# An earlier start of the first q and v products, and attention's scores as three fp32r passes in place of one fp32 product

## The chip, the cores and the metric

The kernel runs on one core of a Trainium2 chip. The metric is the device time of one execution in microseconds (us). The core's engines run their own instruction streams and meet at semaphores: PE (TensorE, the products), DVE (VectorE), ACT (ScalarE), POOL (GpSimd) and SP (SyncE, which only issues transfers here). PEld is PE's loading of weights, shown apart.

## The reference, cut to what matters

An input of 8 batches x 512 rows x 128 goes through four layers: attention, a mixture of 16 experts, a state-space layer, and the experts again. The change is in the first one:

```python
x = x + attn(layernorm(x), w_qkv, w_proj, b_proj)
# attn: q, k, v = split(x @ w_qkv.T); one head of width 128 for the scores
scores = einsum('bqh,bkh->bqk', q, k) * scale      # 512 x 512 per batch
probs  = softmax(scores);  out = probs @ v
out    = out @ w_proj.T + b_proj
# then: x = x + ffn(layernorm(x)), whose router takes the top 4 of 16 experts
```

## The kernel before, in words

All work is ordered by hand: each engine's block is a list of steps, and every step names the semaphores that it waits for. Attention is a software pipeline over the 8 batches (`skewed`, L269): step i, from -1 to 7, holds on every engine the work of four batches at once: the layer norm and the q and v products of batch i+1 (`first`), the scores and softmax of batch i (`second`), the projection and the router's norm of batch i-1 (`third`), and the router's logits, top 4 and weights of batch i-2 (`fourth`). Step -1 is the start-up. Pieces of weight preparation (`prep`) are mixed into steps -1 to 1. After step 7 the expert layer begins (`ffn_all`), which keeps PE busy until the state-space layer.

Since q.k = x Wq' Wk x', one matrix `a_qk` is made once, "q" is `a_qk` times the transposed normed input `xnT` (`q_proj`, L1582), and the scores are one product of 128x128 by 128x512 for each of 4 row blocks r, with `xnT` as the other side (`scores`, L1564). The names by step and engine, in the order of a step's chain:

- DVE: `ln1_stats` (L1050, L1053) of batch i+1, two `maxes` (L1065), `xn_out` (L1059), the third max, `x1_out` (L1075), `router_stats` of i-1 (L1081, L1084), the fourth max, `router_lg` and `router_top` of i-2 (L1103 to L1121), `recip` (L1070), `router_weights` of i-2 (L1128 to L1140), `router_norm` (L1090) and `router_xn` (L1096) of i-1. Then the next step's L1050.
- POOL: `ln1_chain` (L460, L462), which `xn_out` waits for; `add_bias` (L468), which waits for `xn_out`; `router_stash` of i-2 (L454), which writes the low part `ffn_lo` for the expert layer; `router_chain` of i-1 (eight of L434, one of L449), which waits for `router_stats` and which `router_norm` waits for.
- ACT: `router_t` (L659, L661), two `exps` (L623), two `pT` (L629), `xnT_out` (L636), two more `exps`, `q_out` (L641), two `pT`, `router_exp` (L666), `attn_out` (L652), `router_out` (L670), `v_out` (L646).
- PE: scores 0 and 1 (L1569), `router_turn` (L1626), scores 2, `project` (L1617), scores 3, `p_turn` 0 and 1 (L1599), `xn_turn` (L1579), `router_logits` (L1633), `pv` 0 (L1609), `q_proj` (L1584), `p_turn` 2, `v_proj` (L1593), `p_turn` 3, `pv` 1 to 3, `router_parts` (L1639).

The tiles `qT` and `xnT` have two slots, used in turn. At the start, small vectors (biases and the like) come by six small transfers into one row, and a product with a column of ones (L1850) spreads them over the partitions; ACT copies them to `vecs` (L854).

In the start-up step PE's list was, word for word:

```python
xn_turn(0)
eng.wait_ge(w_vecs, 6 * 16)
eng.matmul(bank(2)[:, 0:VEND], ones[0:1, :], vec_row[0:1, 0:VEND], ...).then_inc(prep_ps, 1)
eng.wait_ge(prep_sb, 2)
q_proj(0, 0); prep(0, 0); v_proj(0, 0); prep(0, 1)
```

The functions that the diff touches, and what calls them:

## Time and profile before

| | us |
|---|---|
| median of 3 runs | 724.89 |
| lowest and highest | 724.85, 726.3 |
| the profiled execution's own time | 726.56 |
| its span, from first to last instruction | 724.8 |

Busy shares of the span: PE 98%, PEld 80%, DVE 86%, ACT 79%, POOL 34%. The attention pipeline runs from about 10 to 124 us. The rows further down have the time since the span's start, the duration, the engine, the line, output and inputs, and in brackets the idle time of the engine just before and what ended it. A product's record is longer than the time it keeps PE from the next one, since products are pipelined: what counts is the distance from start to start. An fp32 product leaves two PE records.

### The profile page before, as it was taken

The page shows a single profiled execution, that of the slowest core. Times are in us where ns is not written, and L with a number is a line of the kernel's source. Part 1 is how long each engine was busy: PE and PEld are TensorE (multiplying, and loading weights), DVE is VectorE, ACT ScalarE, POOL GpSimd, SP SyncE. Part 2 cuts the span into 40 slices and gives each one's busy share as a digit, 9 for nine tenths or more (in the row PEclk, how much of TensorE's full clock was granted, in tenths as well). Part 3 has the DMA queues.
Part 4 walks back from the last instruction along what each step waited for, and adds up shares of the span by engine and source line. Part 5 has one row for each costly group of instructions (what it writes and reads, how often), then busy time and mean ns, then how long its engine had stood idle before and what let it go on. Part 6 is the DMA issues. An engine that isn't in the chain of part 4 may idle for free.

```text
span 724.8 us, 13089 instructions
## 1 busy us (share of the span) xinstructions
PE 711.4 (98%) x3826; PEld 580.4 (80%) x3826; DVE 625.4 (86%) x1503; ACT 574.8 (79%) x1097; POOL 242.9 (34%) x389
## 2 busy tenths in 40 slices
PE   8999999999999999999999999999999999999998
PEld 6788787888788877778888888888878887887886
DVE  3678886999999999967689899899889989898996
ACT  2776767988988899778787787777678889888885
POOL 2454564000015100015757767767760000610000
PEclk9999999999999999999999999999999999999999
DMA  9000002654555454300000000000055455555651
GB/s 264 16 2 3 12 30 91 224 191 158 182 189 187 163 172 182 141 0 2 1 1 1 4 3 1 9 4 1 33 202 194 171 194 201 200 189 169 223 198 52
DMA packets 29380, 77.19 MB, mean 106 GB/s; under 512 B 4899, under 2 KB 9726, under 8 KB 29310
## 3 DMA queue, kind: packets, MB, share of 16 engines
q1 hardware_dynamic: 28980, 76.29, 30.9%
q8 instruction: 31, 0.51, 0.3%
q14 instruction: 39, 0.32, 0.1%
q10 hardware_dynamic: 330, 0.08, 0.0%
HBM read 73.73 MB, written 2.62 MB: 105 GB/s over the span
## 4 chain that ended last, share of the span: by engine, by line
PE 49%; DVE 2%; issue 1%; POOL 1%; ACT 1%; DVEq 0%; POOLq 0%; ACTq 0%
PE ps L1701 4%; PE ps L1703 4%; PE ps L1702 4%; PE ps L1733 4%; PE ps L1734 4%; PE ps L1735 4%; PE ps L1950 3%; PE ps L1755 3%; PE ps L1756 3%; PE ps L1757 3%; PE ps L1973 2%; PE ps L2008 2%; PE ps L1959 2%; PE ps L1985 1%; PE ps L1965 1%
## 5 line engine op out<-in xcount | busy, mean ns | idle before, releaser
L712 ACT ACTIVATE s_ring<-ps,b1T 128x512 f32<-128x512 f32 x256 | 171.3, 687 | 35.9 <-PE ps L1735 34.6
L1183 DVE SCALAR_TENSOR_TENSOR s_ring<-s_ring,top_col,r_all 128x1024 f32<-128x1024 f32 x128 | 166.3, 1300 | 19.2 <-ACT s_ring L712 18.4
L1195 DVE TENSOR_TENSOR s_lo<-s_ring,s_hi 128x1024 fp32r<-128x1024 f32 x126 | 153.6, 1219 | 1.9 <-ACT s_hi L718 1.9
L718 ACT ACTIVATE s_hi<-s_ring 128x1024 fp32r<-128x1024 f32 x128 | 135.0, 1055 | 9.9 <-DVE s_ring L1183 8.9
L1701 PE MATMUL ps<-s_hi,w_hi 128*128 128x512 f32 x256 | 101.7, 397 | 2.6 <-DVE s_lo L1195 2.5
L1733 PE MATMUL ps<-ffn_hi,w_hi 128*128 128x512 f32 x256 | 103.7, 405 | 0.2 <-ACT s_ring L712 0.2
L1703 PE MATMUL ps<-s_hi,w_lo 128*128 128x512 f32 x256 | 101.3, 396 | 0.0
L1735 PE MATMUL ps<-ffn_hi,w_lo 128*128 128x512 f32 x256 | 101.2, 395 | 0.0
L1734 PE MATMUL ps<-ffn_lo,w_hi 128*128 128x512 f32 x256 | 101.1, 395 | 0.0
L1702 PE MATMUL ps<-s_lo,w_hi 128*128 128x512 f32 x256 | 100.9, 394 | 0.0
L1701 PEld LDWEIGHTS ps<-s_hi,w_hi 128*128 128x128 f32 x256 | 48.2, 188 | 17.0 <-DVE s_lo L1195 6.2
L527 POOL TENSOR_TENSOR ramp<-upto,dt_a 128x512 f32<-128x512 f32 x32 | 33.0, 1041 | 85.4 <-PE ps L1703 73.8
L1702 PEld LDWEIGHTS ps<-s_lo,w_hi 128*128 128x128 f32 x256 | 48.2, 188 | 11.1
L1735 PEld LDWEIGHTS ps<-ffn_hi,w_lo 128*128 128x128 f32 x256 | 48.0, 188 | 11.3
L1703 PEld LDWEIGHTS ps<-s_hi,w_lo 128*128 128x128 f32 x256 | 48.2, 188 | 11.0
L1733 PEld LDWEIGHTS ps<-ffn_hi,w_hi 128*128 128x128 f32 x256 | 48.2, 188 | 10.7 <-ACT s_ring L712 0.7
L1734 PEld LDWEIGHTS ps<-ffn_lo,w_hi 128*128 128x128 f32 x256 | 48.2, 188 | 9.7
L454 POOL TENSOR_TENSOR ffn_lo<-tT,ffn_hi 128x512 fp32r<-128x512 f32 x16 | 22.5, 1404 | 88.8 <-ACT ffn_hi L661 88.8
L434 POOL TENSOR_TENSOR rt_small<-rt_small,mhalf 128x4 f32<-128x4 f32 x32 | 37.8, 1181 | 2.5
L1260 DVE SCALAR_TENSOR_TENSOR conv_acc<-ps,conv_taps,conv_acc 128x511 f32<-128x511 f32 (+2 forms) x48 | 35.0, 742 | 1.4 <-ACT conv_acc L769 1.3
L434 POOL TENSOR_TENSOR rt_small<-rt_mv,eps 128x4 f32<-128x4 f32 x16 | 7.7, 480 | 81.2 <-DVE rt_mv L1084 80.5
L1973 PEld LDWEIGHTS ps<-xb_tok,gram 128*128 128x128 f32 x256 | 32.9, 192 | 1.9 <-issue 0.5
(267 smaller groups left out, 1559.4 us busy)
## 6 DMA issues: line engine op xcount, KB each, us to landing
r_all<-route_dram SPq DMA_DIRECT2D x128, 512.0 KB, 3.9
out_dram<-X SPq DMA_DIRECT2D x7, 256.0 KB, 4.3
X<-in_L_attn_a_x_dram SPq DMA_DIRECT2D x1, 1536.0 KB, 8.6
rows_f<-route_dram SPq DMA_DIRECT2D x48, 32.0 KB, 3.0
w_rows<-in_L_ffn_mlp_w_dram SPq DMA_DIRECT2D x1, 1024.0 KB, 7.9
route_dram<-route_cols SPq DMA_DIRECT2D x64, 8.0 KB, 1.5
X<-in_L_attn_a_x_dram SPq DMA_DIRECT2D x2, 256.0 KB, 5.5
ssm_rows<-in_L_attn_b_W_in_dram SPq DMA_DIRECT2D x1, 384.0 KB
```

The source lines that it names most:

```text
L434: eng.tensor_tensor(o, a, bb, op).then_inc(R["pool"], 1)
L712: eng.activation(s_ring[q % NR][:, e % 2, :], h_bank(F, b, e), ACT.Silu, bias=b1T[:, e:e + 1], scale=ALPHA).then_inc(F["act"], 1)
L718: eng.activation(s_hi[q % NR][:, :, :], s_ring[q % NR][:, :, :], ACT.Copy).then_inc(F["hi"], 1)
L1183: eng.scalar_tensor_tensor(out=s_ring[q % NR][:, :, :], in0=s_ring[q % NR][:, :, :], scalar=top_col[:, 0:1], in1=r_all[q % NR][:, :, :], o ...
L1195: eng.tensor_tensor(s_lo[q % NR][:, :, :], s_ring[q % NR][:, :, :], s_hi[q % NR][:, :, :].bitcast(F32), ALU.subtract).then_inc(F["lo"], 1)
L1701: eng.matmul(bank(6), w2_hi[:, e, :], hi, start=False, stop=False)
L1702: eng.matmul(bank(6), w2_hi[:, e, :], lo, start=False, stop=False)
L1703: mm = eng.matmul(bank(6), w2_lo[:, e, :], hi, start=False, stop=(e == NE - 1))
L1733: eng.matmul(h_bank(F, b, e), w1_hi[:, e, :], ffn_hi[:, b, :], start=True, stop=False)
L1734: eng.matmul(h_bank(F, b, e), w1_hi[:, e, :], ffn_lo[:, b, :], start=False, stop=False)
L1735: eng.matmul(h_bank(F, b, e), w1_lo[:, e, :], ffn_hi[:, b, :], start=False, stop=True).then_inc(F["h"], 1)
L1973: mm = eng.matmul(bank(3)[:, h * HD:(h + 1) * HD], gram[:, c % 2, h, :], xb_tok[:, c % 2, h // 2, (h % 2) * HD:(h % 2 + 1) * HD], start=Fa ...
```

## The change

Two edits. The first concerns the start-up: PE does three idle products, the first q and the first v product ahead of the small vectors' outer product, and ACT copies q and v ahead of `vecs`. The second concerns the scores of batches 1 to 7: each score product becomes three fp32r passes, high part of q by high part of x, low part of q by high part of x, and high part of q by low part of x. Batch 0 keeps the fp32 product, from a tile of its own (`q_first`). The parts are made by three new operations of 128x512 for each of the batches 1 to 7: ACT `xnT_high` right behind `xnT_out`; POOL `xnT_low` behind `add_bias`; DVE `q_low` behind `router_top`, reading q from PSUM. On POOL, `router_stash` and `router_chain` trade places. `xn_turn` also waits for `q_low` of the batch before.

```diff
@@ POOL
+            def xnT_low(b, par):
+                wait(eng, S1["xnT_hi"], b)
+                wait(eng, S1["scores"], NT * (b - 1))
+                eng.tensor_tensor(xnT_lo[:, par, :], xnT[:, par, :], xnT_hi[:, par, :].bitcast(F32),
+                                  ALU.subtract).then_inc(S1["xnT_lo"], 1)
...
                 if first:
                     ln1_chain(i + 1)
                     add_bias(i + 1)
+                if first and second:
+                    xnT_low(i + 1, 1 - odd)
+                if third:
+                    router_chain(R1, i - 1)
                 if fourth:
                     router_stash(R1, i - 2)
-                if third:
-                    router_chain(R1, i - 1)
@@ ACT
             def q_out(b, par):
                 wait(eng, S1["q_ps"], b + 1)
                 wait(eng, S1["scores"], NT * (b - 1))
-                eng.activation(qT[:, par, :], bank(4), ACT.Copy).then_inc(S1["q"], 1)
+                out = q_first[:, :] if b == 0 else qT[:, par, :]
+                eng.activation(out, bank(4), ACT.Copy).then_inc(S1["q"], 1)
+
+            def xnT_high(b, par):
+                wait(eng, S1["xnT"], b + 1)
+                wait(eng, S1["scores"], NT * (b - 1))
+                eng.activation(xnT_hi[:, par, :], xnT[:, par, :], ACT.Copy).then_inc(S1["xnT_hi"], 1)
...
                     xnT_out(0, 0)
+                    q_out(0, 0)
+                    v_out(0, 0)
                     eng.wait_ge(prep_ps, 3)
                     eng.activation(vecs[:, 0:VEND], bank(2)[:, 0:VEND], ACT.Copy).then_inc(prep_sb, 1)
-                    q_out(0, 0)
                     prep(0, 0)
-                    v_out(0, 0)
                     prep(0, 1)
...
                 if first:
                     xnT_out(i + 1, 1 - odd)
+                    xnT_high(i + 1, 1 - odd)
                 if second:
                     exps(i, 2)
@@ DVE
+            def q_low(b, par):
+                wait(eng, S1["q"], b + 1)
+                wait(eng, S1["scores"], NT * (b - 1))
+                eng.tensor_tensor(qT_lo[:, par, :], bank(4), qT[:, par, :].bitcast(F32), ALU.subtract).then_inc(S1["q_lo"], 1)
...
                     router_top(R1, i - 2)
+                if first and second:
+                    q_low(i + 1, 1 - odd)
                 if second:
                     recip(i)
@@ PE
             def scores(b, par, r):
-                if (b, r) == (0, 0):
+                if (b, r) == (0, 2):
                     eng.wait_ge(prep_sb, 3)
                 wait(eng, S1["q"], b + 1)
                 wait(eng, S1["pT"], NT * (b - 1) + r + 1)
-                eng.matmul(bank(r), qT[:, par, r * P:(r + 1) * P], xnT[:, par, :], start=True,
-                           stop=True).then_inc(S1["scores"], 1)
+                rows = slice(r * P, (r + 1) * P)
+                if b == 0:
+                    eng.matmul(bank(r), q_first[:, rows], xnT[:, par, :], start=True,
+                               stop=True).then_inc(S1["scores"], 1)
+                    return
+                wait(eng, S1["xnT_hi"], b)
+                eng.matmul(bank(r), qT[:, par, rows], xnT_hi[:, par, :], start=True, stop=False)
+                wait(eng, S1["q_lo"], b)
+                eng.matmul(bank(r), qT_lo[:, par, rows], xnT_hi[:, par, :], start=False, stop=False)
+                wait(eng, S1["xnT_lo"], b)
+                eng.matmul(bank(r), qT[:, par, rows], xnT_lo[:, par, :], start=False, stop=True).then_inc(S1["scores"], 1)
 
             def xn_turn(b):
...
                 wait(eng, S1["q"], b)
+                wait(eng, S1["q_lo"], b - 1)
...
                     xn_turn(0)
+                    idle_products(3)
+                    eng.wait_ge(prep_sb, 2)
+                    q_proj(0, 0)
+                    v_proj(0, 0)
                     eng.wait_ge(w_vecs, 6 * 16)
                     eng.matmul(bank(2)[:, 0:VEND], ones[0:1, :], vec_row[0:1, 0:VEND], start=True,
                                stop=True).then_inc(prep_ps, 1)
-                    eng.wait_ge(prep_sb, 2)
-                    q_proj(0, 0)
                     prep(0, 0)
-                    v_proj(0, 0)
                     prep(0, 1)
```

What this makes of POOL's list, in a step from 2 to 6 of the attention pipeline. Before it stands so (ln_ve and ln_rs are the layer norm's chain, X the bias, ffn_lo the stash, rt_small the router's chain, of which the first and last rows are shown):

```order
L460 TENSOR_TENSOR ln_ve<-ln_mv,eps 128x4 [waits attn_xn,attn_aggr]
L462 TENSOR_TENSOR ln_rs<-ln_ve,mhalf 128x4 [waits attn_rstd]
L468 TENSOR_TENSOR X<-X,vecs 128x512 [waits attn_xn]
L454 TENSOR_TENSOR ffn_lo<-tT,ffn_hi 128x512 [waits router1_t,router1_t_hi]
L434 TENSOR_TENSOR rt_small<-rt_mv,eps 128x4 [waits router1_xn,router1_aggr]
...
L449 TENSOR_TENSOR rt_small<-rt_small,rt_mv 128x4 [waits router1_pool]
```

And so after the change, in the changed kernel's line numbers:

```order
L464 TENSOR_TENSOR ln_ve<-ln_mv,eps 128x4 [waits attn_xn,attn_aggr]
L466 TENSOR_TENSOR ln_rs<-ln_ve,mhalf 128x4 [waits attn_rstd]
L472 TENSOR_TENSOR X<-X,vecs 128x512 [waits attn_xn]
L480 TENSOR_TENSOR xnT_lo<-xnT,xnT_hi 128x512 [waits attn_scores,attn_xnT_hi]
L438 TENSOR_TENSOR rt_small<-rt_mv,eps 128x4 [waits router1_xn,router1_aggr]
...
L453 TENSOR_TENSOR rt_small<-rt_small,rt_mv 128x4 [waits router1_pool]
L458 TENSOR_TENSOR ffn_lo<-tT,ffn_hi 128x512 [waits router1_t,router1_t_hi]
```

The router's chain now stands behind the new subtraction, and the stash stands directly behind the chain's last instruction. On ACT, in the same steps, before:

```order
L629 ACTIVATE probsT<-ps 128x512 x2
L636 ACTIVATE xnT<-ps 128x512
L623 ACTIVATE probs,row_sum<-ps,neg_max 128x512 x2
L641 ACTIVATE qT<-ps 128x512
L629 ACTIVATE probsT<-ps 128x512 x2
```

and after:

```order
L641 ACTIVATE probsT<-ps 128x512 x2
L648 ACTIVATE xnT<-ps 128x512
L659 ACTIVATE xnT_hi<-xnT 128x512
L635 ACTIVATE probs,row_sum<-ps,neg_max 128x512 x2
L654 ACTIVATE qT<-ps 128x512
L641 ACTIVATE probsT<-ps 128x512 x2
```

The copy to the high part has come in between `xnT_out` and the third `exps`.

## Rows read from the trace of the kernel before

**Rows 1.** Busy time by window: window, length, each engine's busy us (instructions), PE clock, DMA share, GB/s.

```profile
60.00:80.00 20.00, 20.00 (x137) 15.90 (x136) 17.33 (x78) 14.39 (x35) 11.74 (x19) 1.00 0.02 5
```

**Rows 2.** Timeline of PE in attention's step 5 and in the expert layer.

```profile
70.89 1.88 PE L1569 MATMUL ps<-xnT,qT 128*128 128x512 f32 x4
72.61 0.60 PE L1626 MATMUL ps<-ident,t 128*128 128x128 f32 x4
...
76.56 0.60 PE L1579 MATMUL ps<-ident,xn 128*128 128x128 f32 x4
...
128.11 0.39 PE L1733 MATMUL ps<-ffn_hi,w_hi 128*128 128x512 f32 x1
...
128.80 0.40 PE L1733 MATMUL ps<-ffn_hi,w_hi 128*128 128x512 f32 x1
```

**Rows 3.** Timeline of DVE in step 5.

```profile
72.37 0.87 DVE L1050 BATCH_NORM_STATS2 ln_st<-X 128x6 f32<-128x128 f32 x4
...
75.16 1.11 DVE L1059 TENSOR_SCALAR xn<-X,ln_mv,ln_rs 128x128 f32<-128x128 f32 x4 [0.22 <-POOL ln_rs L462]
...
78.63 0.38 DVE L1084 BATCH_NORM_AGGREGATE rt_mv<-rt_st 128x2 f32<-128x6 f32 x4
...
82.46 0.26 DVE L1128 TENSOR_TENSOR rt_tmp<-rt_tmp 128x64 f32<-128x64 f32 x1 [0.88 <-ACT rt_tmp L666]
...
83.37 1.11 DVE L1090 TENSOR_SCALAR t<-X,rt_mv,rt_small 128x128 f32<-128x128 f32 x4
...
85.66 0.87 DVE L1050 BATCH_NORM_STATS2 ln_st<-X 128x6 f32<-128x128 f32 x4
```

**Rows 4.** Timeline of POOL in step 5.

```profile
77.69 1.26 POOL L454 TENSOR_TENSOR ffn_lo<-tT,ffn_hi 128x512 fp32r<-128x512 f32 x1
79.09 0.20 POOL L434 TENSOR_TENSOR rt_small<-rt_mv,eps 128x4 f32<-128x4 f32 x1
...
83.00 0.20 POOL L449 TENSOR_TENSOR rt_small<-rt_small,rt_mv 128x4 f32<-128x4 f32 x1
```

**Rows 5.** Timeline of ACT in step 5.

```profile
77.27 0.61 ACT L636 ACTIVATE xnT<-ps 128x512 f32<-128x512 f32 x1
...
79.62 0.69 ACT L623 ACTIVATE probs<-ps,neg_max 128x512 f32<-128x512 f32 x1 [1.08 <-DVE neg_max L1065]
```

**Rows 6.** Timeline of POOL from step 6 to 7.

```profile
109.59 0.20 POOL L449 TENSOR_TENSOR rt_small<-rt_small,rt_mv 128x4 f32<-128x4 f32 x1
109.72 0.61 POOL L476 CAST rows_r<-rows_f 80x512 fp32r<-80x512 f32 x1
110.41 1.27 POOL L478 TENSOR_TENSOR rows_r<-rows_f,rows_r 16x512 fp32r<-16x512 f32 x1
```

**Rows 7.** Timeline of DVE beside it.

```profile
110.33 2.20 DVE L1090 TENSOR_SCALAR t<-X,rt_mv,rt_small 128x128 f32<-128x128 f32 x4
...
113.71 1.28 DVE L1065 TENSOR_REDUCE neg_max<-ps 128x1 f32<-128x512 f32 x2
```

**Rows 8.** The line L1090 over the whole span: duration ns min/median/max.

```profile
L1090 DVE TENSOR_SCALAR t<-X,rt_mv,rt_small x64: 333/341/1429, 43.0 to 634.9; 128x128 f32<-128x128 f32 x64
```

**Rows 9.** Timeline of the start-up, all engines.

```profile
7.58 6.64 SPq L295 DMA_DIRECT2D b_rows<-in_L_ffn_mlp_b_dram  x1
...
8.41 0.60 ACT L636 ACTIVATE xnT<-ps 128x512 f32<-128x512 f32 x1 [1.91 <-PE ps L1579]
9.86 0.53 PE L1850 MATMUL ps<-vec_row,ones 1*128 1x156 f32 x2 [1.48 <-DMA scale_col<-in_L_ffn_scale_dram]
...
10.31 1.82 PE L1584 MATMUL ps<-xnT,a_qk 128*128 128x512 f32 x2
...
21.26 0.66 PE L1579 MATMUL ps<-ident,xn 128*128 128x128 f32 x4 [0.42 <-DVE xn L1059]
```

**Rows 10.** Busy time by window (as in rows 1), start-up.

```profile
10.60:14.00 3.40, 3.40 (x12) 2.31 (x12) 0.35 (x1) 1.32 (x3) 1.26 (x1) 0.50 1.06 392
```

**Rows 11.** Transfers issued in the first 25 us: KB each, us to landing.

```profile
b_rows<-in_L_ffn_mlp_b_dram SPq DMA_DIRECT2D x1, 16.0 KB, 10.7
```

More of the change, by code:

```diff
@@ L132, in build @@
             xnT = own("xnT", [P, 2, SEQ])
-            qT = own("qT", [P, 2, SEQ])
+            qT = own("qT", [P, 2, SEQ], F32R)
             probs = own("probs", [P, NT, SEQ])
@@ L142, in build @@
             qkv_rows = own("qkv_rows", [P, 3, D])
+            xnT_hi = own("xnT_hi", [P, 2, SEQ], F32R)
+            xnT_lo = own("xnT_lo", [P, 2, SEQ], F32R)
+            qT_lo = own("qT_lo", [P, 2, SEQ], F32R)
+            q_first = own("q_first", [P, SEQ])
             tap_rows = w1_rows.rearrange("p (k w) d -> p k w d", w=CONV_W)
@@ L221, in build @@
         S1 = {n: sem("attn_" + n) for n in (
-            "stats", "aggr", "rstd", "xn", "xnT_ps", "xnT", "q_ps", "q", "v_ps", "v", "scores", "max", "probs",
+            "stats", "aggr", "rstd", "xn", "xnT_ps", "xnT", "xnT_hi", "xnT_lo", "q_ps", "q", "q_lo", "v_ps", "v", "scores", "max", "probs",
             "pT_ps", "pT", "o_ps", "rec", "o", "y_ps", "xb", "x1")}
```

## Prediction

> **What bounds the kernel now.** I read the page first: PE is busy for 98% of the span, so the first question is whether the attention stage, where the change lies, is bound there too. The windows say yes: between 60 and 80 us PE is busy for 20.00 of 20.00 us at full clock [rows 1]. The timelines of one step then show who else is close. DVE's list for a step begins with L1050 at 72.37 and comes round at 85.66, so a step takes 13.29 us [rows 3]. The reader is to see that DVE is nearly closed as well. Its step runs from L1050 to the router's L1084, ending at 79.01; POOL's chain starts 0.08 us later, at 79.09, and ends at 83.20 [rows 4]; DVE's L1090 starts at 83.37; L1050 follows 2.29 us after that [rows 3]. Between chain and L1090 there are 0.17 us, of which about 0.04 us is what a semaphore takes. So a loop DVE, POOL, DVE of 13.29 - 0.13 = 13.16 us lies right under PE's 13.29 us. Whatever PE saves beyond 0.13 us per step is not seen, and whatever is put into this loop is seen in full. That loop is what I work out below.
>
> **The scores on PE.** Two fp32 score products hold PE from 70.89 to 72.61, so 0.86 us each [rows 2]. Three fp32r passes of the same shape in the expert layer take 128.80 - 128.11 = 0.69 us [rows 2]. That is 0.17 us less per product, 0.68 us per step of four, 4.8 us over seven batches. By the loop above at most 0.13 us a step of it could come out.
>
> **The three new operations.** ACT's copy to the high part is like its other copies of 128x512: 0.61 us [rows 5]. It stands ahead of the third exps; the fourth has an idle 1.08 us in front of it [rows 5], which takes the delay up. DVE's q_low reads 128x512 from PSUM; near 0.68 us by the maxes of that size (two in 1.28 [rows 7]). It comes before recip and the router's weights, where DVE sits idle for 0.88 us waiting for ACT [rows 3], so I cost it at nothing; without that cover it would be 0.6 us a step. POOL's xnT_low is like the stash, 1.26 us [rows 4]. This one has no cover, because POOL's router chain is queued behind it and DVE's router_norm waits for the chain. Its start follows from the row chain: the x transposes begin at 76.56 and end at 77.16 [rows 2], xnT_out ends at 77.88, the high copy, 0.5 us behind it with overlap, at 78.4 [rows 5], so xnT_low runs about 78.5 to 79.75. The chain then starts at 79.8 where it started at 79.09: +0.7 us. PE, being ahead, can bring the transposes forward: xn_out ends at 76.27 [rows 3] and the transposes start at 76.56, so up to 0.2 us; I take 0.15. Net +0.55 us on the chain, +0.4 us on a step, since 0.13 us was slack and some 0.02 us is rounding.
>
> **The stash behind the chain.** In the new order POOL goes on from the chain's last instruction straight to the 1.26 us stash, at the very moment at which DVE is released into router_norm. The trace of before has this situation once. Between steps 6 and 7 POOL follows its chain, ending at 109.79, with a CAST (109.72 to 110.33) and a subtraction that ends at 111.68 [rows 6]. Beside it the four L1090 take 2.20 us [rows 7] where they take 1.11 [rows 3], and the longest single one is 1429 ns against a median of 341 [rows 8]: 110.33 + 1.43 = 111.76, which is 0.08 us past POOL's end. The instruction was held until POOL was through. From POOL's end at 111.68 to DVE's next group at 113.71 it was 2.03 us [rows 7], so I count from POOL's end and not from the chain's.
>
> For a step of the new kernel, in step 5's times: chain ends at 83.20 + 0.55 = 83.75, stash ends at 83.75 - 0.04 + 1.26 = 84.97, the next step's L1050 at 84.97 + 2.03 = 87.0. Against 85.66 that is +1.34 us. Of it 0.4 us is the late chain and 0.94 us is the held norm.
>
> The Trainium skill, "SBUF — State Buffer", "Who interferes with whom", says that a tensor_scalar in a two-port mode and a GpSimd instruction exclude each other for a whole instruction, and that the one issued first wins. By that rule, the trace agrees in the case above, where POOL was first. The same rule would turn round if DVE were first: then POOL's stash waits, which nothing needs soon, and the 0.94 us vanish. It is the second rival.
>
> Bounds for the held norm: below, 0 (a stash that gives way); above, 1.35 us, if DVE's first instruction is held and the rest then starts from scratch as in rows 6 and 7. I take 0.94, since POOL's list needs no semaphore between chain and stash that is still open, while DVE needs one from the chain's end. In step 6 DVE is held already, by the CAST and the subtraction; the stash now stands ahead of both, so this step gets +0.4 for the late chain and +1.2 for the stash in full.
>
> Stash and norm meet in the steps with all four parts, 2 to 6, so five times: 4 x 1.34 + 1.6 = 7.0 us.
>
> **The first steps.** Step 1 has xnT_low ahead of its router chain but no stash: +0.7 us on DVE's entry into step 2. The start-up gains. xnT is there at 9.01, but the q product starts only at 10.31, since the outer product waits 1.48 us for small transfers [rows 9]; it will start at about 9.1. The granted clock was 0.50, the 1.2 GHz level, from 10.6 to 14.0 [rows 10], after PE had stood idle for those 1.48 us; the q product took 1.82 us [rows 9], where the one at full clock is two records 0.43 apart, like a score product. With PE idle for hardly 0.3 us in that place, I expect 2.4 GHz to stay. Then 3.4 us at half clock hold 1.7 us of work, so PE could be 1.2 + 1.7 = 2.9 us early. Not all of it lasts: the second expert weights have landed with b_rows, at 7.58 + 10.7 = 18.28 us [rows 9, 11], and on PE the first four transposes that need them stand ahead of the second transposes of probs and of those of x. A group of four keeps PE for some 0.45 us (0.60 with the tail of the last [rows 2]). So the x transposes of batch 1 (21.26 [rows 9]) can't come before 18.3 + 2 x 0.45 = 19.2 us. I take -2.1 us, bounds -1.2 (only the earlier q) and -2.9.
>
> At the end, step 7 has neither xnT_low nor norm in the loop, and PE's scores and transposes come 0.2 us sooner behind DVE's maxes. The expert layer that follows is the same code, so it is moved and not changed.
>
> **The sum:** -2.1 + 0.7 + 7.0 - 0.2 = +5.4 us on the profiled execution's own 726.56 us (span 724.8), so 732.0. The median of the runs shown is 724.89, 1.67 lower; I put the difference on the median: 730.3 us.
>
> **Rivals.**
>
> First, PE alone sets the pace, as its 100% suggests, and the loop through POOL has slack that I don't see (the norm early enough anyway). Then 0.68 us x 7 and the start-up come out: 724.9 - 4.8 - 2.1 = 718.0. With the loop's floor of 13.16, but without delay, -2.1 - 5 x 0.13 gives 722.2. For it: PE busy without a gap. Against it: the 0.08 and 0.17 us at both ends of POOL's chain [rows 3, 4]. I put the time at 722.
>
> Second, DVE is first at the port, or isn't held: each step costs only the late chain. -2.1 + 0.7 + 5 x 0.4 - 0.2 = +0.4: 725.3. For it: the median of 64 such instructions is 341 ns [rows 8], so few are held. Against: in the one place where POOL has a long instruction directly behind its chain, it was first [rows 6, 7].
>
> Third, the longer step makes PE idle for 14.63 - 12.6 = 2 us a step, in two or three gaps, and the clock falls to the lower level, as it did at the start after 1.48 us. The transposes and q products that the loop passes (about 0.6 + 0.6 us) would take twice as long: +1.0 us in each of five steps: 735.3. For it: rows 9 and 10. Against: the gaps are split between router_turn, the transposes of probs and x, each under 1.48 us.
>
> Fourth, the start-up gives nothing, since DVE and ACT are what batch 1 waits for: 732.4, in my range.
>
> **How the numbers follow.** My forecast 0.60 (its own range 728.3 to 732.6, with the fourth rival in it); not held, 725.3: 0.17; faster by the loop's floor or PE: 0.14; clock: 0.09. The range reaches down to 724.3 to hold most of the second case, and up to 733.5. About 0.2 lies outside. This kernel's measurement can tell about 0.2% (1.4 us) from no change. The second case straddles it: 0.02 faster, 0.11 same, 0.04 slower. With 0.14 faster from the first: faster 0.16, same 0.11, slower 0.73.
>
> **What would show it.** Held norm: L1090's group at 2.0 us or more in steps 2 to 6, its first instruction ending with the stash. Late chain: the first L434 of a step about 0.05 us behind the end of xnT_low. Step length, L1050 to L1050, 14.6 us; 13.7 says the second rival, 13.2 or less the first. PE then has some 2 us idle per step, ahead of router_turn and of the transposes of probs. Start-up: q product at 9.1 us, clock 1.00 through 14 us, x transposes of batch 1 near 19.2. Scores: the passes 0.23 us apart. I am wrong if POOL's stash starts late or DVE's norm keeps its 1.1 us.

## The result: slower by 0.9%

| | before | changed |
|---|---|---|
| median, us (runs) | 725.6 (4) | 732.04 (4) |
| lowest and highest, us | 724.85, 726.74 | 731.84, 732.45 |
| the profiled execution: time, span, us | 726.56, 724.8 | 732.45, 730.7 |

The ratio is 1.0091 with the interval [1.0072, 1.011]. The forecast was 730.3 us, in a range of 724.3 to 733.5. The two profiled spans differ by 5.9 us; the sum had said 5.4.

**The step's loop after the change.** The rows ahead of the prediction call the stretch from 72.37 us on "step 5". It holds the layer norm of batch 5 (its `ln1_stats` is the sixth of eight), so by the count from step -1 it is step 4, and it is called so from here on. DVE's timeline in step 4 (start, us, engine, line, operation, output and inputs, pieces, idle time before). L1069 is `ln1_stats`, L1108 the end of `router_stats`, L1089 the new `q_low`, L1114 `router_norm`, L1120 `router_xn`:

```profile
73.96 0.87 DVE L1069 BATCH_NORM_STATS2 ln_st<-X 128x6 f32<-128x128 f32 x4
...
80.22 0.38 DVE L1108 BATCH_NORM_AGGREGATE rt_mv<-rt_st 128x2 f32<-128x6 f32 x4
...
83.05 0.68 DVE L1089 TENSOR_TENSOR qT_lo<-ps,qT 128x512 fp32r<-128x512 f32 x1
...
85.28 2.11 DVE L1114 TENSOR_SCALAR t<-X,rt_mv,rt_small 128x128 f32<-128x128 f32 x4 [0.46 <-POOL rt_small L453]
87.55 1.11 DVE L1120 TENSOR_SCALAR X<-X,rt_small 128x128 f32<-128x128 f32 x4 [0.15 <-DVE t L1114]
88.57 0.67 DVE L1069 BATCH_NORM_STATS2 ln_st<-X 128x6 f32<-128x128 f32 x3
```

POOL's timeline beside it (L480 is `xnT_low`, L438 and L453 the router's chain, L458 the stash):

```profile
79.98 1.27 POOL L480 TENSOR_TENSOR xnT_lo<-xnT,xnT_hi 128x512 fp32r<-128x512 f32 x1 [0.67 <-ACT xnT_hi L659]
81.21 0.20 POOL L438 TENSOR_TENSOR rt_small<-rt_mv,eps 128x4 f32<-128x4 f32 x1
...
85.05 0.20 POOL L453 TENSOR_TENSOR rt_small<-rt_small,rt_mv 128x4 f32<-128x4 f32 x1
85.25 1.29 POOL L458 TENSOR_TENSOR ffn_lo<-tT,ffn_hi 128x512 fp32r<-128x512 f32 x1
```

From L1069 to L1069 it is 88.57 - 73.96 = 14.61 us, where it was 13.29 [rows 3]. Two links have grown. `router_stats` ends at 80.60, but POOL begins its chain only at 81.21, right at the end of `xnT_low`; before, the two stood 0.08 us apart [rows 3, 4]. And the stash starts at 85.25, 0.03 us ahead of `router_norm`, whose four instructions now take 2.11 us where they took 1.11 [rows 3]. DVE idles ahead of them and waits for POOL.

The line L1114 over the whole span (duration ns min/median/max) answers to [rows 8]:

```profile
L1114 DVE TENSOR_SCALAR t<-X,rt_mv,rt_small x64: 332/341/1415, 41.9 to 640.8; 128x128 f32<-128x128 f32 x64
```

Median and maximum are what they were; how many of the instructions are near the maximum isn't in this row. In the attention stage alone (40 to 110 us, grouped by form) it shows:

```profile
L1114 DVE TENSOR_SCALAR t<-X,rt_mv,rt_small 128x128 f32<-128x128 f32 x20 | 9.8, 546 | 4.1 <-POOL rt_small L453 4.1
```

A mean of 546 ns against 341 is 0.205 x 20 = 4.1 us over five groups of four, of which the one in step 1 has no stash behind its chain. A maximum alone would not have told this.

PE's timeline in the same step (L1601, L1603 and L1605 are the three passes, L1662 `router_turn`, L1635 `p_turn`):

```profile
75.39 0.40 PE L1605 MATMUL ps<-xnT_lo,qT 128*128 128x512 f32 x1
76.79 1.32 PE L1635 MATMUL ps<-ident,probs 128*128 128x128 f32 x8 [1.00 <-ACT probs L635]
...
85.51 0.27 PE L1675 MATMUL ps<-ident,rt_w 128*128 128x128 f32 x1
85.54 0.48 PE L1601 MATMUL ps<-xnT_hi,qT 128*128 128x512 f32 x1
85.85 0.39 PE L1603 MATMUL ps<-xnT_hi,qT_lo 128*128 128x512 f32 x1
...
86.32 0.39 PE L1601 MATMUL ps<-xnT_hi,qT 128*128 128x512 f32 x1
86.55 0.40 PE L1603 MATMUL ps<-xnT_hi,qT_lo 128*128 128x512 f32 x1
...
87.45 0.66 PE L1662 MATMUL ps<-ident,t 128*128 128x128 f32 x4 [0.28 <-DVE t L1114]
```

A score product now takes 86.32 - 85.54 = 0.78 us where it took 0.86 [rows 2]. Besides, the fp32 product ahead of its first pass keeps PE for 85.54 - 85.51 = 0.03 us only; before the change the same product kept PE for 0.11 us (70.78 to 70.89). It is less time on PE, and PE spends it waiting: for the softmax ahead of `p_turn` and for the held norm ahead of `router_turn`. The window that answers to [rows 1] (length, then the busy us of each engine):

```profile
60.00:80.00 20.00, 17.69 (x130) 14.90 (x129) 17.79 (x73) 14.25 (x34) 10.92 (x18) 1.00 0.02 4
```

**The start-up after the change**, PE:

```profile
9.04 1.10 PE L1620 MATMUL ps<-xnT,a_qk 128*128 128x512 f32 x2
...
18.57 0.66 PE L1697 MATMUL ps<-ident,w_rows 128*128 128x128 f32 x4 [1.14 <-DMA b_rows<-in_L_ffn_mlp_b_dram]
...
19.50 0.60 PE L1615 MATMUL ps<-ident,xn 128*128 128x128 f32 x4
```

and the window that answers to [rows 10]:

```profile
10.60:14.00 3.40, 3.40 (x18) 2.17 (x18) 1.26 (x3) 2.05 (x5) 1.27 (x1) 1.00 1.04 380
```

The q product starts at 9.04 instead of 10.31 and takes 1.10 instead of 1.82 us [rows 9]. The granted clock is 1.00 (2.4 GHz) from 9.0 to 10.6 us and in the row above, where it was 0.50 (1.2 GHz) from 10.6 to 14.0 [rows 10]. The x transposes of batch 1 come at 19.50 instead of 21.26, after a wait for the second expert weights.

### The profile page after: what moved, and what is told of

Read it like the earlier page. It is cut to its first block, busy times and chain, and to the rows that moved or that the text cites. A ratio compares the mean times of both kernels' runs of the same rounds, so it can differ in the third digit from the quotient of the medians.

```text
span 730.7 us, 13196 instructions
## 1 busy us (share of the span) xinstructions
PE 709.5 (97%) x3860; PEld 582.7 (80%) x3860; DVE 635.7 (87%) x1510; ACT 579.9 (79%) x1104; POOL 251.7 (34%) x396
## 4 chain that ended last, share of the span: by engine, by line
PE 49%; DVE 2%; issue 1%; POOL 1%; ACT 1%; DVEq 0%; POOLq 0%; ACTq 0%
PE ps L1737 4%; PE ps L1739 4%; PE ps L1738 4%; PE ps L1769 4%; PE ps L1770 4%; PE ps L1771 4%; PE ps L1987 3%; PE ps L1791 3%; PE ps L1792 3%; PE ps L1793 3%; PE ps L2010 2%; PE ps L2045 2%; PE ps L1996 2%; PE ps L2022 1%; PE ps L2002 1%
## 5 line engine op out<-in xcount | busy, mean ns | idle before, releaser
L458 POOL TENSOR_TENSOR ffn_lo<-tT,ffn_hi 128x512 fp32r<-128x512 f32 x16 | 22.6, 1411 | 84.3 <-ACT ffn_hi L679 84.2
L438 POOL TENSOR_TENSOR rt_small<-rt_small,mhalf 128x4 f32<-128x4 f32 x32 | 37.3, 1166 | 2.5
L438 POOL TENSOR_TENSOR rt_small<-rt_mv,eps 128x4 f32<-128x4 f32 x16 | 7.7, 481 | 81.6 <-DVE rt_mv L1108 81.5
```

The lines of the kernel that those rows point to most:

```text
L438: eng.tensor_tensor(o, a, bb, op).then_inc(R["pool"], 1)
```

## The experiments

Ten kernels were run. All ratios are to the kernel before, in runs on the same chip. Where a figure for a step is given, it is the distance of DVE's `ln1_stats` from step 3, 4 or 5 to the next.

**1. The start-up edit alone.** To `before` only these edits (POOL's order and the fp32 scores unchanged):

```diff
@@ ACT
                     xnT_out(0, 0)
+                    q_out(0, 0)
+                    v_out(0, 0)
...
-                    q_out(0, 0)
                     prep(0, 0)
-                    v_out(0, 0)
@@ PE
             def scores(b, par, r):
-                if (b, r) == (0, 0):
+                if (b, r) == (0, 2):
...
                     xn_turn(0)
+                    idle_products(3)
+                    eng.wait_ge(prep_sb, 2)
+                    q_proj(0, 0)
+                    v_proj(0, 0)
                     eng.wait_ge(w_vecs, 6 * 16)
...
-                    eng.wait_ge(prep_sb, 2)
-                    q_proj(0, 0)
                     prep(0, 0)
-                    v_proj(0, 0)
```

> The start-up edit alone on the kernel before. My theory: q product at 9.1 us, PE clock 1.00 through 14 us, x transposes of batch 1 near 19.4 instead of 21.26 us, and the pipeline's steps then PE-bound at 13.3 us as before, so the gain of some 2 us lasts: 1.5 to 2.2 us faster than before. Rival (the start-up gives nothing that lasts, DVE or the transfers are what step 1 waits for): within 0.5 us of before.

Measured: 725.34 us (12 runs) beside 725.24; ratio 0.9997 [0.9984, 1.0011]. The expected 1.5 to 2.2 us weren't there, and the interval leaves room for about 1.2 us at most. In its profile the edit did what it does in the changed kernel: x transposes of batch 1 at 19.56, and the window 10.6 to 14.0 at full clock:

```profile
10.60:14.00 3.40, 3.40 (x19) 2.26 (x18) 1.18 (x2) 2.13 (x5) 1.27 (x1) 1.00 1.04 366
```

So the profile of before was not typical of its own kernel. The executions of before, 63 in the runs of the experiments, fall into two groups by the mean clock over the span: at 0.999 and 1.0 (47 of them) the spans are mostly 721.8 to 723.4 us, at 0.996 to 0.998 (16) they are 723.9 to 727.1. The profiled one, 724.8 at 0.997, is of the second group, and [rows 10] show where it lost its time. The kernel with the edit has both kinds too (3 of its 12 executions at 0.997 or 0.998, with spans of 724.9 to 725.2).

**2. The three passes and the three new operations alone**, with the start-up of before (the edits of experiment 1 taken back out of the changed kernel, on ACT and in the wait of `scores` too):

```diff
@@ PE
                     xn_turn(0)
-                    idle_products(3)
-                    eng.wait_ge(prep_sb, 2)
-                    q_proj(0, 0)
-                    v_proj(0, 0)
                     eng.wait_ge(w_vecs, 6 * 16)
...
+                    eng.wait_ge(prep_sb, 2)
+                    q_proj(0, 0)
                     prep(0, 0)
+                    v_proj(0, 0)
```

> The changed kernel without its start-up edit (q, v and the small vectors' product in the old order). The runs of the start-up edit alone were level with before, so I now expect this one level with the changed kernel, within 1 us of 732, the same steps of 14.6 us, and 6 us slower than before. What I forecast at first (the start-up gives 2 us) would put it near 734.

Measured: 732.91 us (731.06 to 734.19, 5 runs); ratio 1.01 [1.0081, 1.0119]; step 14.62 us. Beside the changed kernel's 732.04 the medians put the start-up edit at some 0.9 us, inside the spread of these five runs. This run also gives a start at full clock without the edit. PE's timeline:

```profile
10.11 0.53 PE L1886 MATMUL ps<-vec_row,ones 1*128 1x156 f32 x2 [1.69 <-DMA scale_col<-in_L_ffn_scale_dram]
10.57 1.12 PE L1620 MATMUL ps<-xnT,a_qk 128*128 128x512 f32 x2
...
19.09 0.66 PE L1697 MATMUL ps<-ident,w_rows 128*128 128x128 f32 x4 [0.82 <-DMA b_rows<-in_L_ffn_mlp_b_dram]
...
20.02 0.60 PE L1615 MATMUL ps<-ident,xn 128*128 128x128 f32 x4
```

PE stood idle for 1.69 us, longer than the 1.48 us of [rows 9], and the granted clock stayed 1.00 from 10.6 to 14.0; the q product took 1.12 us. Counted from each kernel's first `ln1_stats` (3.99 here, 3.88 in the changed kernel), the transposes come 16.03 us later here and 15.62 us later there, 0.4 us apart where the q products are 1.5 us apart. Both starts reach the second weights early and wait for them (0.82 and 1.14 us of idle), and in both the transposes follow 0.93 us behind the end of that wait (19.09 to 20.02, 18.57 to 19.50). So the 0.4 us is the difference in when the weights landed; at like clock the edit's own part is lost in this wait.

The profile of experiment 3, also with the start of before, has the low clock again (0.54 from 10.6 to 14.0 us), behind an idle time of only 1.27 us. The nine kept profiles with the start-up edit all have 1.00 there. Whether the edit makes the low clock rarer is not settled: in experiment 1 it was as frequent (3 of 12) as in before (16 of 63).

**3. Only the stash behind the chain**, in the kernel before:

```diff
@@ POOL
-                if fourth:
-                    router_stash(R1, i - 2)
                 if third:
                     router_chain(R1, i - 1)
+                if fourth:
+                    router_stash(R1, i - 2)
```

> The kernel before with one edit: on POOL router_stash stands behind router_chain. No new operation, scores in fp32. My theory (DVE's router_norm is held while POOL's stash runs): L1090's group of four takes 2.1 us instead of 1.1, first one near 1300 ns, a step takes 83.20 - 0.04 + 1.26 + 2.03 - 72.37 = 14.1 us instead of 13.3, and the kernel is 4 to 5 us slower (about 730). Rival (the engines don't hold each other, the changed kernel's loss is the added subtraction alone): same as before, steps of 13.3 us.

Measured: 729.56 us; ratio 1.0066 [1.0049, 1.0083]; step 14.18 us where it was 13.29. DVE's and POOL's timelines in step 4:

```profile
84.80 2.04 DVE L1090 TENSOR_SCALAR t<-X,rt_mv,rt_small 128x128 f32<-128x128 f32 x4
```

```profile
84.48 0.29 POOL L449 TENSOR_TENSOR rt_small<-rt_small,rt_mv 128x4 f32<-128x4 f32 x1
84.72 1.26 POOL L454 TENSOR_TENSOR ffn_lo<-tT,ffn_hi 128x512 fp32r<-128x512 f32 x1
```

A swap of two neighbours, with no work added, costs 4.3 us: 1.05, 0.97, 0.89 and 0.89 us in steps 2 to 5. The norm's group takes 2.04 us and not 1.11; its first instruction, at 84.80, is held until 86.07, past the stash's end at 85.98. This is the held norm by itself. In step 2 the stash (55.93 to 57.20) meets not the norm but the last instruction of `router_weights`, a tensor_tensor that starts at 56.01: that one takes 1.27 us and not 0.23, and the norm behind it its usual 1.10. So it is not the norm alone that the stash can hold.

**4. The changed kernel, its stash first of the three:**

```diff
@@ POOL
+                if fourth:
+                    router_stash(R1, i - 2)
                 if first and second:
                     xnT_low(i + 1, 1 - odd)
                 if third:
                     router_chain(R1, i - 1)
-                if fourth:
-                    router_stash(R1, i - 2)
```

> The changed kernel with POOL's stash ahead of xnT_low and the router chain. My theory: no hold (L1090's group 1.1 us), but stash, subtraction and chain now stand in a row and the chain starts some 0.7 us later than in the changed kernel, step near 14.3 us, total 1 to 2.5 us faster than the changed kernel. Rival (the order before was free, so it cures the loss): within 1 us of before.

Measured: 729.88 us; ratio 1.0066 [1.0048, 1.0085]; step 14.19 us. The norm's group is back at 1.11 us, but stash (63.81 to 65.10) and `xnT_low` (65.05 to 66.33) now both stand ahead of the chain (66.28). The chain starts 7.79 us behind `ln1_stats` (58.49) where it started 7.25 us behind it: 0.54 of the 1.00 us that the free norm gives goes into the later chain.

**5. The changed kernel, its stash held back until `router_xn` is done** (in the steps that have a `first` part):

```diff
@@ POOL
                 if fourth:
+                    if first:
+                        wait(eng, R1["xn"], NT * i)
                     router_stash(R1, i - 2)
```

> The changed kernel with one wait more: POOL's stash waits until DVE is through with router_norm and router_xn of that step (steps 2 to 6). My theory: the hold goes and only the late chain is left, L1090's group back at 1.1 us, a step takes 13.6 to 13.7 us, 4 to 5.5 us faster than the changed kernel, near 726.5 us, so about level with before. Rival (the late chain is most of the loss): step 14.3 us or more, under 2 us faster than the changed kernel.

Measured: 734.4 us (731.7 to 737.1, the three above 735 at a mean clock of 0.993 to 0.998); ratio 1.0128 [1.0105, 1.0151]; step 14.68 us. The expectation failed, and not over the norm. The timelines of DVE, POOL and ACT, from the norm of step 3 into step 4 (the profiled execution is the one of 731.7 us):

```profile
70.21 1.11 DVE L1116 TENSOR_SCALAR t<-X,rt_mv,rt_small 128x128 f32<-128x128 f32 x4 [0.48 <-POOL rt_small L453]
```

```profile
72.85 1.27 POOL L458 TENSOR_TENSOR ffn_lo<-tT,ffn_hi 128x512 fp32r<-128x512 f32 x1 [2.68 <-issue]
...
79.58 1.27 POOL L480 TENSOR_TENSOR xnT_lo<-xnT,xnT_hi 128x512 fp32r<-128x512 f32 x1 [1.61 <-ACT xnT_hi L661]
```

```profile
74.24 0.69 ACT L679 ACTIVATE tT<-ps,scale_col 128x512 f32<-128x512 f32 x1 [1.79 <-POOL ffn_lo L458]
```

The norm is free: 1.11 us. But the stash reads `tT`, and ACT, which writes it anew in each step, waits 1.79 us for the stash; behind it on ACT stand the softmax and `xnT_out`, for which `xnT_low` and so the chain wait. What the norm gave back was spent through ACT. I had not looked at who waits for the moved stash.

**6. The changed kernel with one fp32 product per score** in place of the three passes. It multiplies the high part of q by the full x, so the low part of q is left out of the scores; the three new operations stay.

```diff
@@ PE
-                eng.matmul(bank(r), qT[:, par, rows], xnT_hi[:, par, :], start=True, stop=False)
...
-                eng.matmul(bank(r), qT_lo[:, par, rows], xnT_hi[:, par, :], start=False, stop=False)
...
-                eng.matmul(bank(r), qT[:, par, rows], xnT_lo[:, par, :], start=False, stop=True).then_inc(S1["scores"], 1)
+                eng.matmul(bank(r), qT[:, par, rows].bitcast(F32), xnT[:, par, :], start=True, stop=True).then_inc(S1["scores"], 1)
```

> The changed kernel with the scores of batches 1 to 7 as one fp32 product again, of the high part of q and x in full (the low part of q is left out of the sum). The three new operations and their waits stay. It gives PE its work of before back. My theory (PE is not the bound, the loop of DVE and POOL is): steps stay at 14.6 us, PE only waits less, within 0.7 us of the changed kernel. Rival (the passes are what costs, by their waits or their number on PE): 3 us or more away from it.

Measured: 732.51 us; ratio 1.0095 [1.0077, 1.0113]; step 14.60 us. Its window of the same stretch:

```profile
60.00:80.00 20.00, 18.60 (x126) 14.14 (x125) 17.77 (x73) 14.27 (x34) 10.89 (x17) 1.00 0.01 3
```

PE is busy for 0.91 us more of these 20 us than with three passes (0.66 us a step), and the time is the same within what can be told. The saving on PE is real and unseen.

**7. An order without the collision:** POOL does stash, `xnT_low` and chain, and `add_bias` comes last; waits hold the stash back until `xn_out` and `add_bias` until `router_xn`, so neither runs beside a norm.

```diff
@@ POOL
                 if first:
                     ln1_chain(i + 1)
-                    add_bias(i + 1)
+                if not third and first:
+                    add_bias(i + 1)
+                if fourth:
+                    if first:
+                        wait(eng, S1["xn"], NT * (i + 2))
+                    router_stash(R1, i - 2)
                 if first and second:
                     xnT_low(i + 1, 1 - odd)
                 if third:
                     router_chain(R1, i - 1)
-                if fourth:
-                    router_stash(R1, i - 2)
+                if third and first:
+                    wait(eng, R1["xn"], NT * i)
+                    add_bias(i + 1)
```

> The changed kernel with another order on POOL: layer norm's chain, stash (behind xn_out), xnT_low, router chain, and add_bias last, behind router_xn. Nothing follows the router chain while DVE does router_norm, and the stash stays early, since the next step's tT waits for it. My theory: no hold (L1090's group 1.1 us), only the late chain left, step 13.6 to 13.7 us, 4 to 5 us faster than the changed kernel, near 727. Rival (something else also grew with the new operations): step above 14 us.

Measured: 726.98 us; ratio 1.0023 [1.0013, 1.0033]; step 13.63 us. The norm's group takes 1.12 us. What is left over 13.29 us is 0.34 us, the chain behind `xnT_low` alone: it starts 7.26 us behind `ln1_stats` (79.44 - 72.18) where it started 6.72.

**8. The same, and the norm waits for less of the chain.** `router_norm` uses only what the first seven of the chain's nine instructions make; only `router_xn` needs all nine.

```diff
@@ DVE, on top of experiment 7
             def router_norm(R, b):
-                wait(eng, R["pool"], 9 * b + 9)
+                wait(eng, R["pool"], 9 * b + 7)
...
             def router_xn(R, b):
+                wait(eng, R["pool"], 9 * b + 9)
```

> The same order, and DVE's router_norm waits for 7 of the router chain's 9 instructions, the last two of which only router_xn needs. That takes two short POOL instructions (0.56 us) out of the loop. My theory: step 13.1 us by the loop, which is then under the 13.3 of before, since PE needs about 12.9: 3 to 4 us faster than the same order without it, level with before or up to 1.5 us faster. Rival (the two short instructions hold DVE instead, or PE's own work is the bound above 13.3): step 13.4 us or more.

Measured: 723.59 us (11 runs) beside 724.84; ratio 0.9979 [0.9969, 0.9988]: faster than the kernel before, by 1.25 us between the medians, and than the changed one, by some 8 us. The step is 13.11 us. DVE and POOL:

```profile
81.73 1.11 DVE L1120 TENSOR_SCALAR t<-X,rt_mv,rt_small 128x128 f32<-128x128 f32 x4
```

```profile
82.02 0.20 POOL L453 TENSOR_TENSOR rt_small<-rt_small,rt_mv 128x4 f32<-128x4 f32 x1
```

The norm starts 0.29 us ahead of the chain's last instruction, with no idle time on DVE before it. And PE's window, with a piece of its timeline:

```profile
60.00:80.00 20.00, 19.97 (x146) 16.90 (x145) 17.85 (x87) 16.00 (x38) 13.06 (x21) 1.00 0.01 3
```

```profile
73.37 0.40 PE L1612 MATMUL ps<-xnT_lo,qT 128*128 128x512 f32 x1
73.74 1.32 PE L1642 MATMUL ps<-ident,probs 128*128 128x128 f32 x8
74.92 0.65 PE L1622 MATMUL ps<-ident,xn 128*128 128x128 f32 x4
```

The same place in the kernel before:

```profile
75.66 1.07 PE L1599 MATMUL ps<-ident,probs 128*128 128x128 f32 x8
```

PE reads as closed, in a step that is 0.18 us shorter than before, and here the cheaper scores show. But PE waits in this step, behind records that are longer than the time they keep it. From start to start the last pass takes 0.37 us and not 0.23, and the eight transposes of probs 1.18 us (73.74 to 74.92) where they took 0.90 before (75.66 to 76.56 [rows 2]). Added up over the step from start to start, PE waits for some 0.46 us. Its work is 12.66 us, 0.65 us less than the 13.31 of before, so the saving on PE is close to the 0.68 us forecast, and PE does not set this step. What does is in experiment 10.

**9. The start-up edit and the early norm in the kernel before**, with its fp32 scores (the edits of experiments 1 and 8, the second in the norm's waits only).

> The kernel before with the start-up edit, and with router_norm waiting for 7 of the chain's 9 instructions; scores as one fp32 product. It asks whether the gain of the last kernel is the earlier norm alone. My theory (without the passes PE is the bound at 13.3 us and the loop of DVE and POOL is under it): steps stay at 13.3 us, level with before, within 0.7 us. Rival (the loop was the bound all along): steps of 13.1 us or less and 1 us or more faster.

Measured: 724.45 us (724.03 to 725.0, 12 runs) beside 724.97; ratio 0.9991 [0.9982, 0.9999]. Its step is 13.31 us (70.29 to 83.58 to 96.90 on DVE, 13.29 and 13.32), and its window is that of [rows 1] again:

```profile
60.00:80.00 20.00, 20.00 (x145) 16.66 (x144) 16.96 (x86) 14.28 (x35) 12.30 (x21) 1.00 0.01 3
```

With fp32 scores the early norm gives nothing in a step: PE holds it at 13.3 us. Against experiment 8 this puts a price on the cheaper scores, with norm and POOL out of the way: 13.31 - 13.11 = 0.20 us a step, and 0.86 us between the medians, which come from different chips.

**10. Two passes instead of three, and the early norm.** High q by low x is left out of the scores, and with it `xnT_low`; POOL's order is that of before.

```diff
@@ POOL
-                if first and second:
-                    xnT_low(i + 1, 1 - odd)
-                if third:
-                    router_chain(R1, i - 1)
                 if fourth:
                     router_stash(R1, i - 2)
+                if third:
+                    router_chain(R1, i - 1)
@@ PE
-                eng.matmul(bank(r), qT_lo[:, par, rows], xnT_hi[:, par, :], start=False, stop=False)
-                wait(eng, S1["xnT_lo"], b)
-                eng.matmul(bank(r), qT[:, par, rows], xnT_lo[:, par, :], start=False, stop=True).then_inc(S1["scores"], 1)
+                eng.matmul(bank(r), qT_lo[:, par, rows], xnT_hi[:, par, :], start=False, stop=True).then_inc(S1["scores"], 1)
```

> The changed kernel with xnT_low and the third pass left out (high part of q by low part of x isn't in the sum), the old order of stash and chain on POOL, and the earlier norm. PE then has some 1.6 us a step less than before, and the loop none of the new work: 13.16 - 0.56 = 12.6 us. My theory (the loop of DVE and POOL sets the step): 12.5 to 12.7 us a step, some 4 us faster than before, near 720.5, and PE idle 0.8 us or more per step. Rival (PE alone sets the step): 11.8 us a step, 9 us faster.

Measured: 723.58 us (722.87 to 725.87, 10 runs); ratio 0.9982 [0.997, 0.9994]: no faster than experiment 8. The step is 13.07 us and not 12.5 to 12.7. Its window, and DVE and POOL round one step (82.24 is the chain's seventh instruction):

```profile
60.00:80.00 20.00, 18.81 (x139) 15.76 (x138) 17.98 (x81) 16.01 (x38) 12.03 (x19) 1.00 0.02 5
```

```profile
72.15 0.87 DVE L1067 BATCH_NORM_STATS2 ln_st<-X 128x6 f32<-128x128 f32 x4
...
74.95 1.12 DVE L1076 TENSOR_SCALAR xn<-X,ln_mv,ln_rs 128x128 f32<-128x128 f32 x4 [0.23 <-POOL ln_rs L466]
...
82.80 0.22 DVE L1163 TENSOR_TENSOR rt_w<-rt_tmp,rt_sum 128x64 f32<-128x64 f32 x1
82.94 1.10 DVE L1112 TENSOR_SCALAR t<-X,rt_mv,rt_small 128x128 f32<-128x128 f32 x4
...
85.23 0.86 DVE L1067 BATCH_NORM_STATS2 ln_st<-X 128x6 f32<-128x128 f32 x4
```

```profile
82.24 0.20 POOL L438 TENSOR_TENSOR rt_small<-rt_small 128x4 f32<-128x4 f32 x1
...
82.80 0.28 POOL L453 TENSOR_TENSOR rt_small<-rt_small,rt_mv 128x4 f32<-128x4 f32 x1
```

PE has over a microsecond to spare in 20 and the step doesn't shrink. The router's chain on POOL doesn't set it either: the seventh instruction, the last that the norm waits for, ends at 82.44, and the norm starts at 82.94, directly behind DVE's own `rt_w`. From 72.15 to 85.23 DVE goes through its list, `q_low` included, and its one wait of more than 0.1 us is the 0.23 us for POOL's `ln_rs`. So the floor of 13.07 us is DVE's own list with that wait, and the expectation of 12.6 us failed because it took the loop through the router's chain for the only bound. Experiment 8 has the same list, with 0.28 us for `ln_rs` in place of 0.23, and stands at 13.11 us: DVE sets it there too. This is read from the two traces; no run took work off DVE. Less work on PE than three passes make is worth nothing here. (The profiled execution, 725.87 us, also had a granted clock of 0.82 between 18 and 22 us and 0.76 between 22 and 26; the other nine ran 722.87 to 725.28 us.)

## Why the prediction was right

The mechanism and the sign were right, and the sum's result close. Term by term, by the profiled executions:

- **The floor.** I put the loop right under PE's step (13.16 us against 13.29), which decided that PE's saving would not be seen. Experiment 6 shows it. The loop's length without the late chain follows from experiments 7 and 4, by taking off what the chain starts later than before: 13.63 - 0.54 = 13.09 and 14.19 - 1.07 = 13.12 us. What the prediction did not see is DVE's own list right beside it, 13.07 us in experiment 10. `q_low`, costed at nothing, did fit into DVE's wait of 0.88 us, but it is part of that list.
- **Late chain.** `ln1_stats` to the chain's first instruction: 6.72 us before (79.09 - 72.37), 7.25 after (81.21 - 73.96): +0.53, where I had +0.55. On the step +0.4 was forecast; the step of experiment 7, which has this part alone, is +0.34.
- **Held norm.** 0.94 us a step forecast; experiment 3, which has this alone, gives 0.89. The two sum to 1.32 in the trace (14.61 - 13.29), where I had 1.34. The Trainium skill, "SBUF — State Buffer", "Who interferes with whom", says that of two such instructions the one issued first wins. In steps 2 to 5 the trace agrees, with the stash at 85.25 and the norm at 85.28 in step 4. Two other rows don't fit, if a record's start is taken for the issue: in step 6 below, a norm instruction starts at 116.31 and POOL's subtraction at 116.38, and DVE is the one held; and in the case from the trace of before, which the prediction read as "POOL was first", L1090 starts at 110.33 and the subtraction at 110.41 [rows 6, 7]. Each of these norm instructions begins while the one before it on DVE is still held or running, so the records can't tell which was first at the port. No run shows a long POOL instruction giving way, my second rival, so what the stash would do then is open.
- **Steps 1 to 6.** From the `ln1_stats` of step 1 (25.97 here, 27.90 before) to that of step 2: +0.84 (forecast +0.7). From there to that of step 6 at 103.17 (98.95 before): +5.31 (forecast 4 x 1.34 = 5.36). Step 6 and 7 together, to the last `x1_out`: +1.23 (forecast 1.6 - 0.2). In step 6 stash, CAST and subtraction lie behind one another on POOL, and three of the norm's four instructions are held, one by each (1.34, 0.63 and 1.42 us), 3.49 us in all. The four together, then the third by itself, and POOL:

```profile
114.49 3.49 DVE L1114 TENSOR_SCALAR t<-X,rt_mv,rt_small 128x128 f32<-128x128 f32 x4 [0.47 <-POOL rt_small L453]
116.31 1.42 DVE L1114 TENSOR_SCALAR t<-X,rt_mv,rt_small 128x128 f32<-128x128 f32 x1
```

```profile
114.46 1.29 POOL L458 TENSOR_TENSOR ffn_lo<-tT,ffn_hi 128x512 fp32r<-128x512 f32 x1
115.69 0.61 POOL L486 CAST rows_r<-rows_f 80x512 fp32r<-80x512 f32 x1
116.38 1.25 POOL L488 TENSOR_TENSOR rows_r<-rows_f,rows_r 16x512 fp32r<-16x512 f32 x1
```

- **PE.** Passes 0.23 us apart as forecast. The first one behind an fp32 product takes 0.31, but the product ahead of it then keeps PE for 0.03 us and not 0.11, so the two even out: by experiment 8 PE saves 0.65 us a step, where I had 0.68. It changed nothing here, since PE isn't the bound. In the three windows from 60 to 120 us PE is busy for 17.69 + 18.70 + 17.07 of 60 us: 1.6 us idle a step by the records, and 14.61 - 12.66 = 1.95 us from start to start, for "some 2". The clock held at 1.00 in all of them, so the third rival is out.
- **The start-up is the term that was mis-sized.** "I take -2.1 us": between the two profiles the `ln1_stats` of step 1 does come 1.93 us sooner, so the arithmetic met the pair of traces. But some 1.5 us of it goes with the clock: counted from the first `ln1_stats` it comes at 24.06 us before, at 22.51 in experiment 2 with the same start at full clock, and at 22.09 after. The low clock of [rows 10] is a property of that execution and not of every one of the kernel: experiment 2 has the old start, a longer idle time ahead of the product, and full clock. What is left at like clock, 0.4 us, is below my bound of 1.2 and belongs to the landing of the second weights. No run shows a lasting gain of the edit (experiment 1: 0.9997). So the time that the fourth rival gave, 732.4, was the nearer one (732.04 measured), though its reason was not: PE waits for the transfer, and not for DVE and ACT. I had put the profile's difference on a median whose executions are mostly of the other kind. The median rose by 6.4 us and not by 5.4, and two of the four runs of before in it are above 726 us; against its medians of 724.84 to 725.24 in the later runs it is about 7. That the forecast missed by no more than 1.7 us is in part luck. Why the clock is low at the start of some executions is not settled here.

The rival "PE alone sets the pace", to which I gave 0.14, is out for the changed kernel, and for experiment 8 too, where PE still waits 0.46 us a step. It holds for the kernel with fp32 scores (experiment 9).

## What to carry to other kernels

When two engines hand a loop to and fro, count the loop against the busiest engine's step before believing that engine's 100%: work taken off it is seen only down to the loop's length, or to that of the next engine's own list. A busy share of 100% can hide waits behind records that overlap, so count from start to start (experiment 8). An instruction that "nobody needs soon" is not free on POOL directly behind the one that releases DVE; put it where DVE runs nothing that it holds up, and look at who waits for the moved instruction (experiment 5). And compare a profile with the spread of its own kernel's runs before taking a stall in it for the kernel's.

## What was not expected of the hardware

- An exchange of two POOL instructions of which neither is new costs 0.7% (experiment 3), since DVE's 0.34 us instruction is held until POOL's 1.26 us one has ended and takes 1.27 us. A tensor_tensor of 0.23 us on DVE was held to 1.27 us in the same way. Short POOL instructions (128x4, 0.20 us) ran beside the norm without a hold on either side (experiment 8, 81.73 to 82.22).
- Of three fp32r passes of 128x512 behind an fp32 product the first holds PE for 0.31 us to the next start, the others for 0.23 us, and the fp32 product ahead holds it for 0.03 us where it held it for 0.11 ahead of an fp32 one.
- The same start-up code ran at either of the clock's two levels: between 10.6 and 14.0 us the granted clock was 0.50 in the profile of before, 0.54 in that of experiment 3 and 1.00 in that of experiment 2, with PE idle for 1.48, 1.27 and 1.69 us ahead of it. The longest idle time was the one without the low clock.
